# A second gather table of whole float32 rows, and float32 one-hots in round 2 of a graph convolution

## What is computed

```python
def gcn_conv(x, W, b, row, col, num_nodes):
    h = x @ W
    loop = jnp.arange(num_nodes, dtype=row.dtype)
    row_sl = jnp.concatenate([row, loop])
    col_sl = jnp.concatenate([col, loop])
    deg = jax.ops.segment_sum(jnp.ones_like(col_sl, dtype=h.dtype), col_sl, num_segments=num_nodes)
    dinv = jax.lax.rsqrt(jnp.maximum(deg, 1.0))
    norm = dinv[row_sl] * dinv[col_sl]
    msg = h[row_sl] * norm[:, None]
    out = jax.ops.segment_sum(msg, col_sl, num_segments=num_nodes)
    return out + b
row, col = (edge_index[0], edge_index[1])
h1 = gcn_conv(emb, W1, b1, row, col, NTOKEN)     # 64 -> 128 features
lookup = gcn_conv(h1, W2, b2, row, col, NTOKEN)  # 128 -> 64 features
return lookup[input]
```

## Time and profile before

| | us |
|---|---|
| median of 3 runs | 9967.49 |
| lowest, highest | 9964.82, 9969.68 |
| the profiled execution's own time | 9966.27 |
| its span in the trace | 9955.3 |
| of it: sorting and first table | 0 to 740 |
| round 1 beside sorting, then chunk 4 alone | 740 to 5091 |
| second table | 5091 to 5137 |
| ring filled for round 2, constant added | 5137 to 5318 |
| visits of round 2 | 5318 to 8844 |
| lookup | 8844 to 9955 |

### The profile page before, as it was taken

One profiled execution on the slowest core, in us unless ns is written; L12 is line 12 of the kernel. 1 busy time (PEld: TensorE's weight loads), 2 busy tenths in 40 slices (PEclk: granted clock), 3 DMA queues, 4 the chain that ended last, 5 costly groups with the idle time before them and its releaser, 6 DMA issues.

```text
span 9955.3 us, 206569 instructions
## 1 busy us (share of the span) xinstructions
PE 4891.4 (49%) x59803; PEld 3495.0 (35%) x59804; DVE 4430.2 (45%) x13350; ACT 2282.7 (23%) x6177; POOL 4582.7 (46%) x4733
## 2 busy tenths in 40 slices
PE   7784665666566566635433445445445445430000
PEld 5432333434333343324323344434434434430000
DVE  8883554555455555544354334334334334330000
ACT  8783443444344344410010000000000000000000
POOL 0004444343444434444534554554554554547777
PEclk9996777777676777755565556555555555565555
DMA  0011111010111101111111111111111111111111
GB/s 11 14 50 25 23 23 24 19 24 20 23 23 23 23 20 23 22 23 24 28 56 21 28 28 24 28 28 24 28 28 24 28 28 33 36 37 49 47 47 46
DMA packets 179454, 281.96 MB, mean 28 GB/s; under 512 B 80796, under 2 KB 93350, under 8 KB 179296
## 3 DMA queue, kind: packets, MB, share of 16 engines
q0 software_dynamic: 151040, 219.19, 10.3%
q1 hardware_dynamic: 17296, 48.30, 1.3%
q10 hardware_dynamic: 10960, 12.62, 0.4%
HBM read 227.84 MB, written 51.96 MB: 28 GB/s over the span
## 4 chain that ended last, share of the span: by engine, by line
PE 35%; issue 34%; DVE 10%; POOL 9%; another core or an unknown queue 8%; DVEq 4%; DMA 0%; ACT 0%; SPq 0%; ACTq 0%; POOLq 0%
PE ps L697 25%; PE ps L611 9%; POOL acc L420 8%; DVE acc L1093 3%; DVE late L1083 2%; DVE hi_onehot L869 1%; DVE place_i L1050 1%; DVE late L1072 1%; DVE acc L929 1%; DVEq L1083 1%; DVEq L929 1%; DVEq L1091 1%; PE ps L751 1%; DVE picked L1044 0%
## 5 line engine op out<-in xcount | busy, mean ns | idle before, releaser
L387 POOL DMA_INDIRECT scratch<-table,source x3920 | 3734.7, 953 | 5022.2 <-PE ps L697 2838.7
L697 PE MATMUL ps<-scratch,late 128*128 x52800 | 3564.5, 224 | 3402.7 <-issue 2749.2
L697 PEld LDWEIGHTS ps<-scratch,late 128*128 128x128 f16 x52800 | 2952.1, 117 | 4378.1 <-issue 4186.7
L1093 DVE TENSOR_TENSOR acc<-acc,ps 128x256 f32 x4400 | 1825.5, 415 | 3606.8 <-remote 2504.2
L1083 DVE TENSOR_SCALAR late<-ramp,target 128x512 f16<-128x512 f16 x3960 | 1434.7, 362 | 99.3 <-PE ps L697 55.9
L611 PE MATMUL ps<-late 125*128 125x440 f16 x4000 | 1298.0, 415 | 288.3 <-issue 183.1
L488 ACT ACTIVATE late<-prt_onehot,scratch 125x128 f16<-125x128 f16 x4000 | 1220.3, 387 | 388.0 <-DVE prt_onehot L869 176.1
L420 POOL DMA_INDIRECT acc<-lookup,ask_i x800 | 845.2, 1057 | 332.0 <-issue 243.6
L583 ACT ACTIVATE acc<-acc,dinv (+1 forms) x196 | 52.2, 336 | 3663.1 <-DVE acc L1093 3592.1
L1072 DVE TENSOR_SCALAR late<-ramp,tcol 125x440 f16<-125x440 f16 x2000 | 668.1, 337 | 179.8 <-remote 179.0
L499 ACT ACTIVATE late<-distance,one_col 128x512 f16<-128x512 f16 x440 | 317.5, 722 | 1808.7 <-remote 1145.3
(11 more groups left out here) (158 smaller groups left out, 976.9 us busy)
## 6 DMA issues: line engine op xcount, KB each, us to landing
scratch<-table,source POOLq DMA_INDIRECT x3920
out<-acc SPq DMA_DIRECT2D x40, 640.0 KB
acc<-lookup,ask_i POOLq DMA_INDIRECT x800
table<-scratch SPq DMA_DIRECT2D x49, 192.0 KB, 1.8
table<-scratch SPq DMA_DIRECT2D x14, 672.0 KB, 3.0
lookup<-acc ACTq DMA_DIRECT2D x49, 128.0 KB
late<-embT ACTq DMA_DIRECT2D x47, 128.0 KB, 2.5
scratch<-edge_index SPq DMA_DIRECT2D x2, 976.6 KB
```

Of the source, the lines that this page charges most:

```text
L387: pool.indirect_dma_start(out=place, out_offset=None, in_=table[r], in_offset=bass.IndirectOffsetOnAxis(ap=source[:, t:t + 1], axis=0)).th ...
L697: last = pe.matmul(visit_ps[k][:, n * FEAT:(n + 1) * FEAT], target_onehot[:, k, n * P:(n + 1) * P], row[:, part * FEAT:(part + 1) * FEAT], ...
L1093: dve.tensor_tensor(dst, dst, visit_ps[k].rearrange("p (n f) -> p n f", f=FEAT), ALU.add).then_inc(visits_added, 1)
```

## The change

Round 2's table holds each row whole, as 64 float32 values (256 bytes for 384). The block-by-block store that followed the scaling of round 2 now follows that of round 1 too: ACT stores a block to the second table once it has scaled it. `split_parts`, `make_table` and SP's 14 stores are gone. POOL waits for the 49 stores on one semaphore, and DVE does so before it adds the constant to `acc`; `find_asked` stands ahead of that wait. In round 2 the gathered rows and the one-hots are float32, the one-hots in another part of `scratch`, and a visit is four matmuls of the program for twelve. Round 1 and its table are as they were.

```diff
-        table = [nc.dram_tensor(f"table{r}", [P * NT, 3 * FEAT], BF16).ap() for r in range(2)]
+        table = [nc.dram_tensor("table0", [P * NT, 3 * FEAT], BF16).ap(), nc.dram_tensor("table1", [P * NT, FEAT], F32).ap()]
...
+        whole_rows = scratch[:, 0:RINGT * FEAT].bitcast(F32).rearrange("p (k f) -> p k f", k=RINGT)
+        whole_onehot = scratch[:, RINGW:RINGW + RING * BN].bitcast(F32).rearrange("p (r n) -> p r n", r=RING)
+        places = gath, whole_rows
+        onehot_of = target_onehot, whole_onehot
...
-            for p in range(PIECES):
-                sp.wait_ge(part_lo, GROUPS + p + 1)
-                sp.dma_start(table_v[1][:, p * PT:(p + 1) * PT, :],
-                             split[:, p % SPLITS, :, :, :].rearrange("p t c f -> p t (c f)")).then_inc(second_written[p % SPLITS], 16)
...
-                    for b in range(SPLITS):
-                        pool.wait_ge(second_written[b], 16 * len(range(b, PIECES, SPLITS)))
+                    pool.wait_ge(second_written, 16 * NB)
...
-                            gather(gath[:, place, :], c * GT + b * W8 + k, batch)
+                            gather(places[r][:, place, :], c * GT + b * W8 + k, batch)
...
-            with act.Fori(0, NB) as n:
-                scale_block(0, n, dtmp, scaled)
-            split_parts()
...
+            def store_block(table, n, step, written):
+                act.wait_ge(step, n * BT + BT)
+                act.dma_start(table[:, bass.ds(n * BT, BT), :], acc[:, bass.ds(n * BT, BT), :]).then_inc(written, 16)
+
+            for r, by, step, to, written in ((0, dtmp, scaled, table_v[1], second_written),
+                                             (1, dinv, lookup_scaled, lookup_v, lookup_written)):
+                scale_block(r, 0, by, step)
+                with act.Fori(1, NB) as n:
+                    scale_block(r, n, by, step)
+                    store_block(to, n - 1, step, written)
+                store_block(to, NB - 1, step, written)
...
-                row = gath[:, bass.ds(place, 1), :].rearrange("p a f -> p (a f)")
+                row = places[r][:, bass.ds(place, 1), :].rearrange("p a f -> p (a f)")
+                parts = 1 if r else 3
                 for n in range(BT):
-                    for part in range(3):
+                    for part in range(parts):
                         last = pe.matmul(visit_ps[k][:, n * FEAT:(n + 1) * FEAT],
-                                         target_onehot[:, k, n * P:(n + 1) * P],
+                                         onehot_of[r][:, k, n * P:(n + 1) * P],
                                          row[:, part * FEAT:(part + 1) * FEAT],
-                                         start=(part == 0), stop=(part == 2))
+                                         start=(part == 0), stop=(part == parts - 1))
...
-                dve.tensor_scalar(target_onehot[:, k, :], ramp[:, :], target[:, bass.ds((g - r * BATCHES) * W8 + k, 1)], None,
+                dve.tensor_scalar(onehot_of[r][:, k, :], ramp[:, :], target[:, bass.ds((g - r * BATCHES) * W8 + k, 1)], None,
                                   ALU.is_equal).then_inc(target_onehots, 1)
...
             dve.wait_ge(visits_added, BATCHES * W8 + CREDIT)
-            make_table()
             find_asked()
+
+            dve.wait_ge(second_written, 16 * NB)
             add_constant(1, b2_rep, BATCHES * W8)
```

More of the change, by code:

```diff
@@ L38 @@
 HALF = CODE // 2
-PIECES, PT = 14, NT // 14
 SPLITS = 4
@@ L66 @@
 assert NT % BT == 0 and CV <= 512 and CB * W8 * CHUNKS == EC and CB < VB
-assert PIECES * PT == NT and OUT_GROUPS * OUT_GROUP == OUT_TILES and OUT_SLOTS * OUT_GROUP <= NT
+assert OUT_GROUPS * OUT_GROUP == OUT_TILES and OUT_SLOTS * OUT_GROUP <= NT
 assert P * NT * BN < CODE * CODE and GB % RINGB == RINGB // 2 and VB == GB + LAG and GB == CB - 1 and LAG * W8 == NB - 1 and LAG == AHEAD
@@ L70 @@
 assert W8 % BT == 0 and RINGT <= P and CHUNKS * GB * P < 1 << 15
-assert CB % 2 == 0 and GROUPS == CB - 1 and LOOPED * SPLITS + 4 == CB - 2 and PT >= BT
+assert CB % 2 == 0 and GROUPS == CB - 1 and LOOPED * SPLITS + 4 == CB - 2
 def dve_rank(k):
@@ L107, in build @@
             for at in (64, 128))
-        SPN = PT * FEAT
+        SPN = BT * FEAT
         split = scratch[:, 0:SPLITS * 3 * SPN // 2].bitcast(BF16).rearrange(
-            "p (b t c f) -> p b t c f", b=SPLITS, t=PT, c=3)
+            "p (b t c f) -> p b t c f", b=SPLITS, t=BT, c=3)
         rest = scratch[:, SPLITS * 3 * SPN // 2:SPLITS * 5 * SPN // 2].bitcast(F32).rearrange(
-            "p (b t f) -> p b t f", b=SPLITS, t=PT)
+            "p (b t f) -> p b t f", b=SPLITS, t=BT)
         ramp8 = sb("ramp8", [P, NB, W8], F16)
@@ L282, in build @@
         first_written = [sem(f"first_written{b}") for b in range(SPLITS)]
-        second_written = [sem(f"second_written{b}") for b in range(SPLITS)]
+        second_written = sem("second_written")
         ask_step = sem("ask_step")
@@ L306, in landed @@
             return gathered[b % 2], TILE_BATCH * ((r * CHUNKS + c) * PER_CHUNK + b // 2 + 1)
-        def tiles_of(p):
-            return acc[:, p * PT:(p + 1) * PT, :]
         block = ctx.enter_context(nc.Block())
@@ L468, in _ @@
             act.activation(dtmp[:, :], deg[:, :], ACT.Sqrt).then_inc(root_taken, 1)
[L470 to L481, removed]
             def scale_column(s, j, b):
@@ L583, in scale_block @@
                     act.activation(tile, tile, ACT.Copy, scale=by[:, bass.ds(n * BT + k, 1)]).then_inc(step, 1)
-            def store_block(n):
-                act.wait_ge(lookup_scaled, n * BT + BT)
-                act.dma_start(lookup_v[:, bass.ds(n * BT, BT), :], acc[:, bass.ds(n * BT, BT), :]).then_inc(lookup_written, 16)
-            with act.Fori(0, NB) as n:
-                scale_block(0, n, dtmp, scaled)
-            split_parts()
[L593 to L597, removed]
+            def store_block(table, n, step, written):
[8 more added lines that the diff above has]
+                store_block(to, NB - 1, step, written)
             lp, lt = (NODES - 1) % P, (NODES - 1) // P
@@ L931, in add_constant @@
                 dve.wait_ge(constant_added, (r + 1) * NT)
-            def make_table():
-                for p in range(PIECES + 2):
-                    if p < PIECES:
-                        dve.wait_ge(part_hi, GROUPS + p + 1)
-                        dve.tensor_tensor(rest[:, p % SPLITS, :, :], tiles_of(p), split[:, p % SPLITS, :, 0, :],
-                                          ALU.subtract).then_inc(rest_hi, 1)
-                    if p >= 2:
-                        b = (p - 2) % SPLITS
-                        dve.wait_ge(part_mid, GROUPS + p - 1)
-                        dve.tensor_tensor(split[:, b, :, 2, :], rest[:, b, :, :], split[:, b, :, 1, :],
-                                          ALU.subtract).then_inc(part_lo, 1)
             step = chain(base_step)
```

## The result

| | before | after |
|---|---|---|
| median of 4 runs, us | 9968.58 | 10154.49 |
| lowest, highest | 9964.82, 9977.37 | 10153.17, 10157.69 |
| profiled execution, its span | 9966.27, 9955.3 | 10153.4, 10142.3 |

The changed kernel takes 1.0185 of the time before (95% interval 1.0173 to 1.0198). The forecast was 10158 us, which is 191 us more than the median of 9967.5 that it started from.

A forecast was written before the change was run, and what follows sets the result against it. Bound: a pattern of waits, PE and POOL nearly taking turns in round 2. From 9966.3 us, - 41 + 1 (table stage) + 231 (round 2) gave 10157, plus 1.2 for the median: 10158; range 9850 to 10450.

The forecast's parts named there:

- The table stage: Between the rounds: 45.1 us from last scaling to first gather become 4, a gain of 41 us, less 1 us allowed.
- The pairs: Round 2 on PE: 64 float32 pairs of weight load and matmul at 0.213 us, 13.65 us a batch, loss 231 us.
- The clock: TensorE in round 2: granted clock stays at the lower level, 0.50 or 1.2 GHz, for the whole round.
- The weakest step: The assumption that TensorE runs at the lower clock, 1.2 GHz, throughout round 2.
- Rival A: Round 2: busy PE raises the clock, 13.1 us a batch with gathers, 7.0 without, 9737 us in all; chance 0.18.
- Rival B: Round 2: instructions cannot wait ahead, PE's array runs dry, 18.8 us for 231 batches, 11345 us in all; chance 0.10.
- POOL and DVE: Round 2: both hide behind PE's 13.65 us; POOL waits 3.6 us a batch, DVE needs at most 6.9 us.
- the gathers stay at 1.25 us each: POOL in round 2: gathers keep starting 1.25 us apart, as the lookup's with rows of 256 bytes do.
- this is the gain that the slow stretches could give: PE in round 2: about 154 instructions a batch for 234, helping where PE is short of instructions, not array time.
- the partial form of B: Round 2 with the array running dry only in part: 15 us a batch, 4065 us for the round, 10469 in all.

The follow-up runs named there:

- e10_twice_by_turns: Changed kernel, but the second and fourth of round 2's five chunks stream every row twice (128 columns for 64): 9993.16 us, 1.0020 of the kernel before.
- e1_columns_twice: Changed kernel, but every float32 matmul of round 2 streams the row twice (128 columns for 64): 6854.87 us, 1.0032 of the kernel before.
- e5_small_rows_16bit: Changed kernel's table and gathers, but twelve 16 bit matmuls per visit on upper half words, values meaningless: 6808.0 us, 0.9951 of the kernel before.
- the two-part kernel: Kernel before with two 16 bit parts a row for three in both rounds, coarser result: 9467.24 us, 0.9496 of the kernel before.
- e6_before_again: The kernel before, unchanged, run again for its trace: 9979.1 us.
- e2_two_parts: Kernel before without the low part's matmul in round 2, table and gathers unchanged: 6836.17 us, 1.0006 of the kernel before.

## Why the prediction was right

**The table stage: right, a little too small.** Forecast were a first gather near 5095, a first visit near 5278 and a gain of 41 - 1 us; measured 5091.1, 5271.7 and 46.2. From the last scaling's end (5087.92 + 0.33) to the first gather it is 2.85 us instead of 4. In this execution round 1 also ended 2.8 us earlier than in the profiled one of before, which the term did not hold and which lies within the 12 us by which the runs of before differ.

**The pairs: right, their explanation not.** A pair takes 0.2133 us against the 0.213 that came from five float32 matmuls of another stage; with 17600 of them a batch is 13.65 us, with gathers and without. But the prediction said that half of the 0.213 is the weight load and the other half the columns. At the lower clock a pair is 0.214 us with 128 columns and 0.213 with 64 (e10_twice_by_turns); at the upper clock it is 0.112 us with 128 and was 0.11 with 64, though there on 64 rows. Had load and columns added up, the doubled columns would have shown. So the columns hide behind the rest of the pair, and the only other thing in it that the trace names is the weight load. No term of the sum rested on that sentence, but a reader who believed it would expect twice the columns to cost time.

**The clock: right, and now with its reason.** The weakest step, 0.50 throughout, held. It had been a choice between rows that disagreed, and only e10_twice_by_turns turned its hint, the share of columns, into a cause. Rival A expected the clock to rise because PE would be busy without a break; the stretch that it pointed to was not quite that, with PE busy for 58.01 of 72 us. Here PE is busy for 3750 of 3750 us and the clock stays at 0.50; with 128 columns behind each weight load it is busy for 75% of a chunk and the clock is 0.85. The Trainium skill ("TensorE: Matmul & The Clock Gate", section "What's actually happening") says that activity releases the throttle. These two rows say that a PE that the profile calls busy can be one that does not release it. Rival A's price was close: it had 13.1 us for a batch with gathers and 9737 us in all; round 2 of e10_twice_by_turns is 176 us shorter than the changed kernel's, 88 for each doubled chunk, and three more would put the doubled kernel at 9993 - 3 x 88 = 9729 us on the long kind. That is an estimate, since e1_columns_twice never ran there.

**No dry array: right.** Rival B would have shown gaps within batches. PE's idle time in round 2 is zero. DVE still starts late there; its additions in round 2 of the changed kernel, on the long kind and then on the short one:

```profile
L1063 DVE TENSOR_TENSOR acc<-acc,ps 128x256 f32 x2199 | 915.2, 416 | 2018.6 <-PE ps L680 1564.5 <-issue 453.4 <-DVE acc L1063 0.3
...
L1063 DVE TENSOR_TENSOR acc<-acc,ps 128x256 f32 x2198 | 915.2, 416 | 1991.5 <-PE ps L680 1991.3 <-DVE acc L1063 0.2
```

The 453.4 us "in issue", which wait for nothing that the trace shows, are there on the long kind alone, and they cost nothing. PE's pair of 0.213 us is long enough to outlast the slow issue.

**POOL and DVE: right where they are hidden.** POOL was to wait some 3.6 us a batch for PE:

```profile
  PE ps L680: 1269.6, 229
```

This is the line of POOL's gathers from 5276 to 8845 that names PE: 1269.6 us in 229 waits, 5.5 each. Leaving out the first, up to 136.5 us long while the ring is full, the rest are (1269.6 - 136.5) / 228 = 5.0. The forecast of 3.6 was for a batch in step, such as the one whose POOL row has 3.78 at 5709.68; the chunks' gatherless batches add longer waits. DVE's one-hot takes 496 ns (480 forecast, and under the 600 that would have mattered).

**One sentence was wrong and hidden:** "the gathers stay at 1.25 us each". Gathers beside the float32 one-hots last 0.98 us on the mean instead of 0.95. In the changed kernel PE's 13.65 us cover that. In e1_columns_twice nothing does:

```profile
L385 POOL DMA_INDIRECT scratch<-table,source x1919 | 1877.8, 979 | 610.8 <-issue 544.6 <-DMA scratch<-table,source 59.8 <-PE ps L680 6.4
```

POOL is the bound there (6.4 us of waiting for PE), and 979 - 953 ns, the mean of e5_small_rows_16bit, times 1919 are 50 us. On the two chips that ran both kernels, the doubled one takes 53 and 55 us more (6852.53 - 6799.43 and 6853.27 - 6798.72). So the longer gathers are most of the reason why the faster matmuls still end at 1.003. That the float32 writes of DVE lengthen them is not shown: PE's float32 reads changed with them, and no run isolated either.

**What the prediction did not see** is that its 14.27 us for a batch of the kernel before hold on one kind of chip. There the change removes a stall of PE (by moving the bound to PE's array) and pays 231.8 us. On the other kind there is no stall to remove, and the same 13.65 us replace 8.9: 1268 us more in all, the gain at the table included. The sentence "this is the gain that the slow stretches could give" was also too hopeful: a third fewer matmuls gave 0.45 us a batch. And the prediction's range did not hold the partial form of B, as it says: that form came to 10469 us, and the range ended at 10450.

**Open.** Why gathers in flight hold up PE and DVE on one kind of chip and not on the other; no trace here names it. Neither the doubled columns in all chunks nor e5_small_rows_16bit ran on the long kind, and the two-part kernel did not run on the short one. No version of full precision was found that beats the kernel before on the short kind. On the long kind the two-part kernel beats both, at the price of a coarser row.

## What to carry to other kernels

Count float32 matmuls by their weight loads: behind a load of 128 by 128, 64 columns or 128 cost the same here (more were not tried), and with the 64 the clock stayed at its lower level although the engine was busy without a break. Read the granted clock beside the busy share. And where one engine seems to stall for nothing that the trace shows, measure both kernels on a second chip before pricing a change by that stall: here the same two kernels differ by 1.9% on one chip and by 18.6% on another.

## What the runs showed of the hardware

- The same kernel took 9977 us on one chip and 6832 on others. Its gathers of 384 bytes a row last 0.95 us in round 2 on either (e6_before_again, e2_two_parts), and a float32 pair takes 0.213 us at the lower clock on either; 1289 us of PE's idle time before the visits of round 1 in the changed kernel lie "in issue" on the one and not on the other.
- In the changed kernel's lookup a gather lasts 1.06 us on the mean on the long kind and 0.95 on the short kind.
- A float32 matmul with 128 columns and one with 64 both take two pairs; a pair is 0.213 us with 64 columns and 0.214 with 128 at 1.2 GHz, and 0.112 us with 128 columns at 2.4 GHz.
- Indirect gathers of 256 bytes a row go out every 1.25 us, as those of 384 bytes do.
- A gather is longer beside other work of DVE: 1.41 us instead of 0.94 for the first two of round 2 in the changed kernel, while DVE computes on 800 elements per partition. In the doubled chunks a gather lasts 0.98 us on the short kind (e1_columns_twice), for 0.95 beside 16 bit work (e5_small_rows_16bit).
